# Laying out the split matrix E with its four contraction blocks innermost, in a convolution-as-lambda kernel

## The reference, cut to what matters

```
keys    = xf @ Wk.T ; softmax_keys = softmax(keys, axis=1)
values  = batch_norm(xf @ Wv.T)                       # b m v
queries = batch_norm((xf @ Wq.T)...)                  # b k n h
content_lambda   = einsum('bmk,bmv->bkv', softmax_keys, values)
position_lambdas = einsum('nmk,bmv->bnkv', E, values)
out = x + einsum('bknh,bkv->bhvn', queries, content_lambda)
        + einsum('bknh,bnkv->bhvn', queries, position_lambdas)
```

## Time and profile before

| what | value |
|---|---|
| median of 3 executions | 1433.52 us (1433.46 to 1433.7) |
| the profiled execution's own time | 1433.76 us |
| its span, first to last instruction | 1432.0 us |
| PE busy | 1418.7 us, 99%, 14740 instructions |
| PEld (weight loads) busy | 1190.8 us, 83% |
| DVE, ACT, POOL busy | 828.9 us (58%), 725.3 us (51%), 432.7 us (30%) |
| granted TensorE clock, mean | 0.999 of full speed |

### The profile page before, as it was taken

The page is one execution under the profiler, slowest core; times in us unless marked ns, Lnnn a source line. Parts: engine busy times, 40 slices in busy tenths (PEclk is TensorE's granted clock), DMA queues, the critical chain, the costliest instruction groups (busy, mean ns, idle before and its releaser), DMA issues.

```text
span 1432.0 us, 36828 instructions
## 1 busy us (share of the span) xinstructions
PE 1418.7 (99%) x14740; PEld 1190.8 (83%) x14740; DVE 828.9 (58%) x1276; ACT 725.3 (51%) x1109; POOL 432.7 (30%) x368
## 2 busy tenths in 40 slices
PE   8999999999999999999999999999999999999998
PEld 8997878888888888888888888888888888888887
DVE  8999865555555555555555555555555555555554
ACT  6784645544544445544554445445444455445542
POOL 6682123232223322232223222322233222322230
PEclk9999999999999999999999999999999999999999
DMA  9833334334234433343344333443344333433431
GB/s 310 285 136 80 73 83 91 79 89 94 67 80 95 95 81 67 87 95 82 65 95 95 82 79 77 91 92 69 81 95 94 82 66 88 95 79 67 95 88 16
DMA packets 475808, 134.73 MB, mean 94 GB/s; under 512 B 339984, under 2 KB 471168, under 8 KB 475264
## 3 DMA queue, kind: packets, MB, share of 16 engines
q1 hardware_dynamic: 473664, 134.18, 39.8%
q10 hardware_dynamic: 2112, 0.13, 0.1%
HBM read 109.12 MB, written 25.17 MB: 94 GB/s over the span
## 4 chain that ended last, share of the span: by engine, by line
PE 98%; DVE 1%; issue 0%; ACT 0%; DMA 0%; POOL 0%; DVEq 0%
PE ps_a L1344 82%; PE ps_b L1357 5%; PE ps_a L1330 4%; PE ps_b L1221 4%; PE ps_a L1211 2%; PE ps_b L1281 0%; DMA x_main<-in_x 0%; DVE v_shift L1040 0%; PE ps_b L1198 0%; DVE bn L761 0%; PE ps_b L1298 0%; DVE v_mv L1027 0%; PE ps_a L1188 0%; ACT q_nat L573 0%; PE ps_b L1233 0%
## 5 line engine op out<-in xcount | busy, mean ns | idle before, releaser
L1344 PE MATMUL ps_a<-v_hi,e_hi 128*128 128x512 f32 x1710 | 668.6, 391 | 0.0
L1344 PE MATMUL ps_a<-v_hi,e_lo 128*128 128x512 f32 x1710 | 665.5, 389 | 0.0
L695 ACT ACTIVATE q_diag<-q_blk,q_shift_n,q_scale_n 128x256 f32<-128x256 f32 x512 | 409.9, 865 | 125.3 <-PE ps_b L1357 121.5
L608 ACT ACTIVATE e_hi<-e_nat 128x512 fp32r<-128x512 f32 x305 | 193.8, 636 | 476.5 <-PE ps_a L1344 199.0
L1344 PE MATMUL ps_a<-b_lo,e_hi 128*128 128x512 f32 (+1 forms) x978 | 380.0, 389 | 0.0
L1344 PEld LDWEIGHTS ps_a<-v_hi,e_hi 128*128 128x128 f32 x1710 | 321.3, 188 | 67.0
L1344 PEld LDWEIGHTS ps_a<-v_hi,e_lo 128*128 128x128 f32 x1710 | 321.3, 188 | 65.5
L1344 PE MATMUL ps_a<-t_lo,e_hi 128*128 128x512 f32 x732 | 285.3, 390 | 0.0
L518 POOL TENSOR_TENSOR e_nat<-e_nat,s_buf 128x512 f32<-128x512 f32 x61 | 98.1, 1608 | 617.4 <-DVE e_lo L792 617.4
L792 DVE TENSOR_TENSOR e_lo<-e_nat,e_hi 128x512 fp32r<-128x512 f32 x305 | 222.0, 744 | 52.2 <-ACT e_hi L608 52.2
L1344 PEld LDWEIGHTS ps_a<-b_lo,e_hi 128*128 128x128 f32 x978 | 183.6, 188 | 38.0
(11 more groups left out here) (144 smaller groups left out, 986.4 us busy)
## 6 DMA issues: line engine op xcount, KB each, us to landing
e_nat<-in_L_conv_E SPq DMA_DIRECT2D x128, 512.0 KB, 3.8
res<-in_x SPq DMA_DIRECT2D x128, 128.0 KB, 3.9
out_dram<-res SPq DMA_DIRECT2D x124, 128.0 KB, 2.6
x_main<-in_x SPq DMA_DIRECT2D x24, 512.0 KB, 6.3
q_dram<-q_nat SPq DMA_DIRECT2D x4, 2048.0 KB, 8.5
q_blk<-q_dram SPq DMA_DIRECT2D x32, 256.0 KB, 3.1
x_more<-in_x SPq DMA_DIRECT2D x8, 512.0 KB, 9.4
out_dram<-res SPq DMA_DIRECT2D x4, 64.0 KB, 2.7
```

The source lines that it names most:

```text
L608: nc.scalar.activation(e_hi[:, i], e_source(i), ACT.Copy).then_inc(e_hi_ready, 1)
L695: ins = nc.scalar.activation(to[:, n], of, ACT.Identity, bias=q_shift_n[:, n:n + 1], scale=q_scale_n[:, n:n + 1])
L1344: ins = nc.tensor.matmul(BANK_OF[odd][i][:, cols] if to is None else to, e[:, i, j].rearrange("p n k -> p (n k)"), v[:, j, cols], start=(( ...
```

## The change

The two tensors keep their size, and their dimensions are reordered: the block index j, which was outside the 128 columns (n, k), becomes the innermost. Column c of block j of a slot now lies at element 4c + j, so the columns of one block stand 4 elements, 16 bytes, apart. `by_block` gives the elementwise instructions a view in the old order, so that the source, which keeps its layout, is read as before: each of them now writes (and, for the subtraction, also reads e_hi) with a step of 16 bytes along the columns. The weight loads read 128 elements with the same step. No instruction, wait, transfer or buffer is added or taken away.

```diff
-        e_hi = sb("e_hi", [P, NP, MJ, TN, KD], f32r)
-        e_lo = sb("e_lo", [P, NP, MJ, TN, KD], f32r)
+        e_hi = sb("e_hi", [P, NP, TN, KD, MJ], f32r)
+        e_lo = sb("e_lo", [P, NP, TN, KD, MJ], f32r)
...
+        def by_block(t):
+            return t.rearrange("p n k j -> p j n k")
...
-                pool.tensor_tensor(e_lo[:, FIRST_SLOTS[0][n]], first_block(n), e_hi[:, FIRST_SLOTS[0][n]].bitcast(f32),
+                pool.tensor_tensor(by_block(e_lo[:, FIRST_SLOTS[0][n]]), first_block(n), by_block(e_hi[:, FIRST_SLOTS[0][n]]).bitcast(f32),
...
-                ins = nc.scalar.activation(e_hi[:, FIRST_SLOTS[p][n]], first_block(n), ACT.Copy)
+                ins = nc.scalar.activation(by_block(e_hi[:, FIRST_SLOTS[p][n]]), first_block(n), ACT.Copy)
...
-                nc.scalar.activation(e_hi[:, i], e_source(i), ACT.Copy).then_inc(e_hi_ready, 1)
+                nc.scalar.activation(by_block(e_hi[:, i]), e_source(i), ACT.Copy).then_inc(e_hi_ready, 1)
...
-                nc.vector.tensor_tensor(e_lo[:, i], e_source(i), e_hi[:, i].bitcast(f32),
+                nc.vector.tensor_tensor(by_block(e_lo[:, i]), e_source(i), by_block(e_hi[:, i]).bitcast(f32),
...
-                            ins = nc.tensor.matmul(bank, e[:, slot, j % MJ].rearrange("p n k -> p (n k)"), v,
+                            ins = nc.tensor.matmul(bank, e[:, slot, :, :, j % MJ].rearrange("p n k -> p (n k)"), v,
...
-                                               e[:, i, j].rearrange("p n k -> p (n k)"), v[:, j, cols],
+                                               e[:, i, :, :, j].rearrange("p n k -> p (n k)"), v[:, j, cols],
```

More of the change, by code:

```diff
@@ L798, in first_lo @@
                 dve.wait_ge(e_hi_ready, p * NP + (n + 1 if n < 3 else NP))
-                nc.vector.tensor_tensor(e_lo[:, FIRST_SLOTS[p][n]], first_block(n), e_hi[:, FIRST_SLOTS[p][n]].bitcast(f32),
+                nc.vector.tensor_tensor(by_block(e_lo[:, FIRST_SLOTS[p][n]]), first_block(n), by_block(e_hi[:, FIRST_SLOTS[p][n]]).bitcast(f32),
                                         ALU.subtract).then_inc(e_lo_ready, 1 if n < 3 else 4)
```

## The result

The changed kernel takes 1487.35 us (median of 4 executions, 1486.88 to 1489.43) against 1433.49 us for the kernel before beside it: ratio 1.038, 95% interval [1.0367, 1.0393]. The forecast was 1444 us, its range 1432 to 1578: the direction and the range hold, the size does not. The loss is 54 us, not 10. That the range holds is owed to rival 1, up to which it was drawn, and not to the forecast's own sum, whose high end was 1463.

The account below looks back on a forecast made before the run. The prediction took TensorE, mostly the matmuls of product, to bound the kernel. It summed 1433.8 + 3.6 (loads after queries) + 6 (stall over the splits) + 1.0 (start) = 1444 us, range 1432 to 1578.

Parts of the forecast that it names:

- rival 1: Weight loads become the bound at 246 ns, 19.6 more than a matmul's 226.7: 1545 us; chance 0.22.
- What bounds the kernel: In the loop TensorE never waits; product's matmuls hold 82% of the span, one starting every 226.7 ns.
- The weight loads: Stepped loads take 216 ns, covered by a matmul's 226.7, so the step costs nothing in the stream.
- own range: Range of the forecast's own sum: 1436.4 us with almost no stall, to 1463 with the high ends.
- its own sign: Forecast is wrong if the matmuls' distance moves at all, or L608 and L792 grow by under 0.44 us.
- Rival 2: Stepped loads take lines from the values' stream: 266.7 ns per matmul, 40 more, 1655 us; chance 0.18.
- Rival 3: Not slower: loads stay covered, splits cost less than 0.44 us more, chain never late, 1434 to 1436 us; chance 0.22.
- Rival 4: Faster: spreading the loads' pieces takes away the matmul's remainder, 60 us less, 1374 us; chance 0.04.
- Loads after queries: First load after queries is uncovered: 34 places at 0.107 us more each, 3.6 us.
- The splits: ScalarE's copies and VectorE's subtractions into E each take 0.47 us more, making the refill chain 2.9 us later.
- the stall: Ahead of product 5, lateness of 2.9 us exceeds the allowed 2.7 by 0.2 in each of 30 loop bodies: 6 us.
- The start: Four GpSimd subtractions ahead of the first matmuls with E, 0.40 us more each, less 0.56 of waiting: 1.0 us.

Follow-up runs that it names:

- e11: Kernel before with matmuls of 512, 384, 256 and 128 columns in product's blocks 0 to 3, TensorE alone loading weights with a 16-byte step: 1475.08 us.
- e15: Kernel before, every product matmul reading one value element 512 times, TensorE alone loading weights with a 16-byte step: 1472.06 us.
- e5: Kernel before, TensorE alone reading its weights with a step of 8 bytes (wrong elements, same work): 1461.64 us, ratio 1.0196.
- e13: Kernel before, every product matmul reading one value element 512 times, with contiguous weight loads: 1380.95 us.
- e14: Kernel before, every product matmul reading one value element 512 times, TensorE alone loading weights with an 8-byte step: 1381.62 us.
- e2: Changed kernel's layout, other engines writing and reading with the 16-byte step, but TensorE loading contiguous weights (wrong elements): 1437.8 us, ratio 1.0037 to the kernel before.
- e12: Against the kernel before, all slots and blocks innermost, so a block's columns stand 112 bytes apart for all engines: 1489.79 us, ratio 1.0386.
- e9: Kernel before with matmuls of 512, 384, 256 and 128 columns in product's blocks 0 to 3, weight loads contiguous: 1165.9 us.
- e6: Kernel before, TensorE alone reading its weights with a step of 12 bytes (wrong elements): 1475.48 us, ratio 1.0298.
- e16: Kernel before with 64 unused bytes after e_lo, moving the values against E's parts: 1445.07 us, ratio 1.0083.
- e18: Kernel before with 32 unused bytes after e_lo, moving the values against E's parts: 1466.1 us, ratio 1.0232.
- e3: Against the kernel before, e_hi and e_lo interleaved element by element, a step of 8 bytes for all engines: 1466.7 us, ratio 1.0236.

## Why the prediction was wrong

1. *What bounds the kernel.* Right: it is TensorE alone, before and after. In the loop every other engine stayed hidden.
2. *The weight loads.* The step that failed is the one that priced the load at "213 ns, and with the 3 ns of hand-over 216 ns" and went on "So in the stream the step costs nothing". Two things were wrong. The floor of such a load is 233 ns (e11, e15, and the 256 columns after the change). That is over the 226.7 of a matmul, and alone makes 6.4 x 5418 = 35 us. And the matmul's 226.7 ns was taken as a fixed sum, though 10 ns of it are the disturbance between the two readings, which the step changes: at 8 bytes, with a short load, it costs 5.3 ns (e5). Together they make (235.7 - 226.6) x 5418 = 49 us, against nothing in the sum. The argument from the earlier trace rows (columns and load of 107 ns side by side, the same 13.3 ns left) held the remainder for a constant of the form; but with still values the matmuls of 256 columns fall to 112 ns, close to the load's own bound of 110, and those of 512 to 216.4 (e13). Equal remainders in two rows didn't show a constant. The prediction's own bounds for the load, 207 to 244 ns, also reached past the 226.7 of a matmul, and its "from 237 ns on" doesn't follow from its figures, by which a load costs from 226.7 on; so its "own range" (whose low end 1436.4 isn't added up either) left out a case that its bounds allowed. By its own sign, that it is wrong if the distance of the matmuls moves at all, it is wrong by 9 ns.
3. *The rivals.* Rival 1 had half of this mechanism, with a price of 246 ns for the load where 233 were measured. Rival 2 was right that the reading of the weights can cost time of the stream (e5 against e14) and wrong in its rule: 16, 32, 64 and 96 lines gave 228.4, 226.6, 231.9 and 234.1 ns. Rival 3 was right that the chain over the splits isn't late (e2), and left the loads at nothing like the forecast. Rival 4 was right that most of the remainder can vanish, but not by spreading the loads.
4. *Loads after queries*, 3.6 us: no run has this term by itself. Of the 47.2 us of 29 bodies, 29 x 14 products x 0.111 us = 45.1 lie in the products; 2.1 us are left, 0.07 per body where 0.107 was forecast.
5. *The splits.* The durations were close: a copy and a subtraction took 0.52 and 0.47 us more in the changed kernel, 0.50 and 0.37 in e2, for 0.47 forecast. By the forecast's formula the lateness is 2.6 us in e2, just under the slack of 2.7, and the 6 us of stall didn't occur. In the changed kernel the slower TensorE should leave the chain more time, which is argued and not measured. e12, with dearer splits, has the stall where it was forecast, so the chain was read rightly. With a margin of 0.2 us either way, the forecast couldn't know on which side it would fall.
6. *The start*, 1 us forecast, about 4 measured (e2). GpSimd's subtraction cost 0.29 us more, less than assumed, but the chain that matters there is that of pairs 3 and 4, where the splits have no slack, and it wasn't walked through: it ends in TensorE's one wait for an evacuation, 1.69 us in e2 and 1.16 in the changed kernel. The prediction's estimate of about 1.9 us for GpSimd's subtraction was too high; it takes 1.57.

That the change came out slower, as forecast, was in part luck: the largest term of the forecast's 10 us, the stall, didn't occur, the two others came to some 6 to 8 us in place of 4.6, and the 49 us that decide stood at nothing.

The SBUF page of the Trainium skill (SBUF — State Buffer, section Specifications), weighed ahead of the result as speaking against the change, was right about the step of 16 bytes: copies rose from 0.64 to 1.15 us, the load's floor from 110 to 233. At 8 bytes, two elements to a line, the copies stayed near the old price (0.68 us) and so did the load (recorded at 193 ns), as it says.

Another page of the Trainium skill (TensorE: Matmul & The Clock Gate, section Step-by-step: what each phase is for) states that loading the next weights doesn't take SBUF read bandwidth from the running matmul. For this form e5 and e14 contradict it: the step of 8 bytes in the loads costs 5.3 ns per matmul with moving values and nothing with still ones. The measurement decides.

*Still open:* why the floor at 16 bytes is 233 and at 112 bytes 227 ns, where twice 107 would be 213; and by what rule of addresses or alignment the two readings collide. Which part of the 9.1 ns is the floor and which the disturbance can't be split cleanly, as both act at once: with the stream still, 6.4 remain; with the load shortened, 4 to 6.

## What to carry to other kernels

A small remainder on every matmul need not be a constant: before pricing anything against it, let the moving operand stand still, and see what is left. When one operand's read is slowed, measure its floor, and compare it with the time of the instruction that covers it; a cover of 5% is decided by nanoseconds that a neighbouring row of another engine does not give. And know where the hot operands lie: 16 unused bytes in front of the values cost this kernel 2.4%.

## What the hardware showed that was not expected

- A load of 128 float32r columns needs 110 ns contiguous (e9), at most 119 with a step of 8 bytes between columns (e14), 174 with 12 (e6), 233 with 16 (e15) and 227 with 112 (e12).
- Matmuls of 512 columns run 216.4 ns apart when they read one value again and again (e13), and 226.6 to 233.0 with contiguous loads and moving values, by the place of the tensors in SBUF alone (e16 to e18).
- Copies on ScalarE and subtractions on VectorE with a step of 16 bytes take 1.8 and 1.6 times as long (1152 and 1210 ns). With 8 bytes the copies take 1.06 times as long (676 ns) and the subtractions no longer than before (739 ns, e3).
